# Attention-and-DHT kernel: small parameters in one packed transfer issued behind the last head, 48 instead of 64 head-dimension rows of q and k, and the low parts of the second half's relative terms subtracted on GpSimd

## The reference, cut to what matters

```python
B, H, W, C = 4, 16, 16, 192; NH = 12; HD = 16; WS = 14; MLP = 768
h = layernorm(x, ln1_g, ln1_b)                       # padded to 28 x 28, cut into 14 x 14 windows
q, k, v = split(h @ qkv_w + qkv_b)                   # 12 heads of 16 dims
rel_h = einsum('bhwc,hkc->bhwk', q, Rh)              # Rh, Rw: rel_pos_h, rel_pos_w by offset
rel_w = einsum('bhwc,wkc->bhwk', q, Rw)
scores = einsum('bqd,bkd->bqk', q, k) * HD**-0.5 + rel_h[..., :, None] + rel_w[..., None, :]
o = softmax(scores) @ v
x1 = x + (o @ proj_w + proj_b)
out = x1 + gelu(layernorm(x1, ln2_g, ln2_b) @ fc1_w + fc1_b) @ fc2_w + fc2_b
# layer 1: Hartley transform, two block-diagonal complex layers (w1, b1, w2, b2), soft threshold,
# transform back, plus the input
```

## Time and profile before

| | us |
|---|---|
| median of 3 runs | 191.21 |
| the profiled execution, its own time | 190.22 |
| its span, first to last instruction | 188.4 |
| PE busy | 175.3 |
| DVE busy | 112.9 |
| ACT busy | 87.5 |
| POOL busy | 65.7 |

### The profile page before, as it was taken

How to read it: one execution, slowest core, us unless ns; L and a number is a source line. 1 busy time by engine, 2 the same in 40 slices (tenths; PEclk the granted TensorE clock), 3 DMA queues, 4 the chain that set the end, 5 groups by cost and what they waited for, 6 DMA issues and landing times.

```text
span 188.4 us, 4169 instructions
## 1 busy us (share of the span) xinstructions
PE 175.3 (93%) x1502; PEld 153.3 (81%) x1502; DVE 112.9 (60%) x303; ACT 87.5 (46%) x230; POOL 65.7 (35%) x120
## 2 busy tenths in 40 slices
PE   7999999997998797899999999999999999999892
PEld 7766996696786675788877996878999999789892
DVE  6729675598888677587755776520111466779532
ACT  3496554934387666587785204554100223071300
POOL 1633439936055456431999521900000000000000
PEclk9999999999699999999999999999999999999999
DMA  5791227976939999957051300000012170000015
GB/s 161 210 221 25 89 79 205 225 204 180 185 105 187 218 213 205 209 115 239 12 155 41 129 0 0 0 3 0 3 43 83 42 171 0 2 0 3 0 31 138
DMA packets 12958, 19.45 MB, mean 103 GB/s; under 512 B 5197, under 2 KB 9695, under 8 KB 12938
## 3 DMA queue, kind: packets, MB, share of 16 engines
q0 software_dynamic: 3392, 10.98, 24.4%
q1 hardware_dynamic: 8810, 7.75, 17.5%
q10 hardware_dynamic: 736, 0.46, 0.9%
HBM read 6.79 MB, written 1.57 MB: 44 GB/s over the span
## 4 chain that ended last, share of the span: by engine, by line
PE 70%; DMA 9%; DVE 7%; SPq 5%; ACT 3%; issue 2%; POOL 0%; ACTq 0%; DVEq 0%; POOLq 0%
PE bank L1632 9%; PE bank L1649 8%; PE bank L1406 6%; PE bank L1474 5%; PE bank L1667 4%; DMA qop<-arena 4%; PE bank L1392 3%; SPq L607 3%; PE bank L1381 3%; PE bank L1488 3%; PE bank L1600 3%; DMA q_last<-maxt 3%; PE bank L1659 3%; PE bank L1446 3%; DMA xt<-in_x_tok 2%
## 5 line engine op out<-in xcount | busy, mean ns | idle before, releaser
L1190 DVE TENSOR_REDUCE negmax<-bank 98x2 f32<-98x392 f32 (+1 forms) x72 | 34.7, 525 | 8.8 <-PE bank L1446 8.7
L1474 PE MATMUL bank<-qop,kop 128*98 128x196 f32 (+4 forms) x140 | 22.6, 262 | 0.1
L951 ACT ACTIVATE arena<-bank 98x392 f32<-98x392 f32 x48 | 21.2, 489 | 2.5 <-PE bank L1474 2.2
L1446 PE MATMUL bank<-kop,qop 126*98 126x196 f32 x80 | 16.4, 294 | 5.3 <-DMA qop<-arena 3.8
L1474 PEld LDWEIGHTS bank<-qop,kop 128*98 128x98 f32 (+4 forms) x140 | 18.8, 176 | 0.9 <-issue 0.9
L1632 PE MATMUL bank<-h2t,wf 96*128 96x512 f32 x72 | 17.4, 398 | 0.4 <-ACT h2t L978 0.4
L1446 PEld LDWEIGHTS bank<-kop,qop 126*98 126x98 f32 x80 | 11.1, 175 | 7.3 <-issue 5.7
L1632 PEld LDWEIGHTS bank<-h2t,wf 96*128 96x128 f32 x72 | 13.3, 188 | 3.9 <-issue 0.6
L1649 PE MATMUL bank<-wf,arena 128*128 128x192 f32 x96 | 15.8, 326 | 0.0
L1649 PEld LDWEIGHTS bank<-wf,arena 128*128 128x128 f32 x96 | 15.7, 190 | 0.1
L1269 DVE TENSOR_TENSOR arena<-bank,arena 128x384 f32<-128x384 f32 x4 | 2.2, 556 | 22.1 <-PE bank L1649 22.1
(11 more groups left out here) (172 smaller groups left out, 379.5 us busy)
## 6 DMA issues: line engine op xcount, KB each, us to landing
kop<-arena POOLq DMA_DIRECT2D x20, 173.0 KB, 5.5
qop<-arena POOLq DMA_DIRECT2D x10, 227.5 KB, 6.7
qop<-arena SPq DMA_DIRECT2D x10, 130.0 KB, 2.5
qop<-arena POOLq DMA_DIRECT2D x10, 130.0 KB, 6.0
arena<-in_relw SPq DMA_DIRECT2D x2, 441.0 KB, 5.1
xt<-in_x_tok SPq DMA_DIRECT2D x4, 192.0 KB, 3.5
scratch<-arena SPq DMA_DIRECT2D x4, 192.0 KB, 2.0
k_last<-arena POOLq DMA_DIRECT2D x4, 173.0 KB, 4.8
```

Of the source, the lines that this page charges most:

```text
L951: nc.scalar.activation(pg[:, e], src[0:HWIN, 0:2 * WIN], ACT.Exp, scale=HD ** -0.5).then_inc(emptied(key), 1)
L1190: nc.vector.tensor_reduce(negmax[0:rows, n % 2, at:at + cols], ps(key)[0:rows, 0:cols * width].rearrange("p (t k) -> p t k", t=cols), AX.X ...
L1446: ins = mm(ps(key)[0:HWIN, WIN * t:WIN * t + WIN], qo(h)[0:126, c0:c0 + HWIN], ko(h)[0:126, WIN * u:WIN * u + WIN], start=True, stop=True)
L1474: ins = mm(ps(key)[0:rows, at:at + n], ko(h)[:, c0:c0 + rows], rhs, start=True, stop=True)
```

## The change

1. The 17 parameter DMAs of SP are gone. The host packs ln2, fc1_b, half4, b1, b2, w1, w2 and w2 turned into one array `params` [128, 20 + 12*24]; POOL loads it by one DMA right behind the last head's r, then `wf1_raw` and `pb`, without waiting for the last head's loads; behind that wait come `wf1_f32`, `f2b` and both rows of b2 in one DMA. Waits on `late_in` become waits on `params_in`, `pb_in` or `late_in`, each for what is used.
2. q and k have 48 rows instead of 64: the high part of q twice and the low part once, k's high and low parts and the high part again. Rows 48 to 63 are zeros: POOL sets `blank` (16 rows), and SP copies it into those rows of all five buffers of `kop` and `qop` by two DMAs before the constant rows of q, and behind a wait for `bv_in`; rows 48 to 63 of `k_last` and `q_last` are copied from there by two more DMAs between those of L611 and L612. Low times low is no longer part of the scores.
3. The relative terms of the second half: ACT writes, besides the high part, an exact copy from the bank to where the low part belongs; POOL subtracts the high part in place, one instruction over 84x1040 for each axis, the first behind `q_low_by_pool`, the second behind head 5's r. DVE's `rel_low` for f = 1 is gone.
4. `kept_busy(3)` instead of `kept_busy(6)` before `max_rows(1)`.

```diff
         def q_rows(h, part):
             f, j = h // HH, h % HH
-            src = q2[j:j + HH * (HD - 1) + 1:HH, f, part, None, :].to_broadcast([HD, 2, QN])
-            return raw(qo(h)[32 * part:32 * part + 32]), raw(src)
+            if part == 0:
+                src = q2[j:j + HH * (HD - 1) + 1:HH, f, 0, None, :].to_broadcast([HD, 2, QN])
+                return raw(qo(h)[0:32]), raw(src)
+            return raw(qo(h)[32:48]), raw(q2[j:j + HH * (HD - 1) + 1:HH, f, 1, :])
...
             sp.dma_start(relw[:, 1], a["relw"][:, 1]).then_inc(relw_in[1], 16)
+            sp.wait_ge(blank_set, 1)
+            sp.wait_ge(bv_in, 16)
+            sp.dma_start(raw(kop[48:64]), raw(blank[:, None, :].to_broadcast([16, OWN, KN]))).then_inc(blank_in, 16)
+            sp.dma_start(raw(qop[48:64]), raw(blank[:, None, 0:QN].to_broadcast([16, OWN, QN]))).then_inc(blank_in, 16)
             sp.wait_ge(qrows_set, 1)
...
-                if 2 <= h < 8:
-                    for dst, src in later_inputs[3 * (h - 2):3 * (h - 2) + 3]:
-                        sp.dma_start(dst, src, allow_slow_non_contiguous=True).then_inc(late_in, 16)
                 if h == 1:
                     sp.wait_ge(*is_full(("rel", 1, 1, 1)))
                     sp.wait_ge(q_lowered, 4)
                     sp.dma_start(raw(k_last[64:128, :]), raw(kop[64:128, 0])).then_inc(krows_set[OWN], 16)
+                    sp.dma_start(raw(k_last[48:64, :]), raw(kop[48:64, 0])).then_inc(krows_set[OWN], 16)
+                    sp.dma_start(raw(q_last[48:64, :]), raw(qop[48:64, 0])).then_inc(qrows_copied, 16)
                     sp.dma_start(raw(q_last[120:126, :]), raw(qop[120:126, 0])).then_inc(qrows_copied, 16)
...
+            nc.gpsimd.memset(raw(blank), 0.0).then_inc(blank_set, 1)
             pool.wait_ge(set_up, 6)
...
+            def r_low_by_pool(axis):
+                for p in range(2):
+                    pool.wait_ge(*is_read(("rel", 1, axis, p)))
+                nc.gpsimd.tensor_tensor(relc[:, 1, axis, 1], raw(relc[:, 1, axis, 1]), raw(relc[:, 1, axis, 0]),
+                                        ALU.subtract).then_inc(r_lowered, 1)
...
-                for copy in range(2):
-                    pool.dma_start(raw(ko(h)[32 * copy:32 * copy + 32]),
-                                   raw(k2[j:j + HH * (HD - 1) + 1:HH, f])).then_inc(k_loaded[h % NOK], 16)
+                pool.dma_start(raw(ko(h)[0:32]),
+                               raw(k2[j:j + HH * (HD - 1) + 1:HH, f])).then_inc(k_loaded[h % NOK], 16)
+                pool.dma_start(raw(ko(h)[32:48]),
+                               raw(k2[j:j + HH * (HD - 1) + 1:HH, f, 0])).then_inc(k_loaded[h % NOK], 16)
...
                         for g in range(3):
                             q_low_by_pool(g)
+                        r_low_by_pool(0)
+                    if h == OWN:
+                        r_low_by_pool(1)
                     if OWN <= h + 1 < NH:
                         load_k(h + 1)
...
+            pool.dma_start(params[:], a["params"]).then_inc(params_in, 16)
+            for c in range(2):
+                pool.dma_start(wf1_raw[:, c], a["fc1_w"][CF * c:CF * c + CF, :]).then_inc(wf1_in, 16)
+            pool.dma_start(pb[:], a["proj_b"].partition_broadcast(128)).then_inc(pb_in, 16)
             for i in range(NOP):
                 pool.wait_ge(r_loaded[i], 16 * len(range(i, HH, NOP)))
             for h in range(NH - NOK, NH):
                 pool.wait_ge(k_loaded[h % NOK], 32 * (h // NOK + 1))
-            pool.wait_ge(late_in, 17 * 16)
-            for c in range(2):
-                pool.dma_start(wf1_raw[:, c], a["fc1_w"][CF * c:CF * c + CF, :]).then_inc(wf1_in, 16)
             for c in range(2):
                 pool.dma_start(wf1_f32[:, c], a["fc1_w"][CF * c:CF * c + CF, :]).then_inc(wf1_again, 16)
+            pool.dma_start(f2b[:], a["fc2_b"].partition_broadcast(128)).then_inc(late_in, 16)
+            pool.dma_start(b2r.rearrange("p x c -> p (x c)"),
+                           a["b2"].rearrange("x n o -> (x n o)").partition_broadcast(128)).then_inc(late_in, 16)
...
                 for src, dst in rel_pieces(axis, ps(key)[0:84, :], p, relc[:, f, axis, 0]):
                     ins = nc.scalar.copy(dst, src)
-                ins.then_inc(r_high, 1)
+                if f == 0:
+                    ins.then_inc(r_high, 1)
+                else:
+                    for src, dst in rel_pieces(axis, ps(key)[0:84, :], p, relc[:, f, axis, 1]):
+                        ins = nc.scalar.copy(raw(dst), src)
+                    ins.then_inc(emptied(key), 1)
...
                 if (n, u) in K_STEPS:
                     k_low(1, K_STEPS.index((n, u)))
-                if (n, u) in R_STEPS:
-                    rel_low(1, *divmod(R_STEPS.index((n, u)), 2))
...
                         if h == OWN:
-                            pe.wait_ge(qrows_copied, 32)
+                            pe.wait_ge(qrows_copied, 48)
...
-                        pe.wait_ge(krows_set[h % NOK], 16 if h % NOK == OWN else 1)
+                        pe.wait_ge(krows_set[h % NOK], 32 if h % NOK == OWN else 1)
...
                 if h == 1:
-                    kept_busy(6, ps(key))
+                    kept_busy(3, ps(key))
...
             pe.wait_ge(qrows_copied, 16)
+            pe.wait_ge(blank_in, 32)
             for n in range(NH + 3):
```

More of the change, by code:

```diff
@@ L362, in build @@
         assert QF_AT == relw_at + 2 * WS * 84 and QF_AT + QN + KN <= vaug_at - 4 * 3 * 128
+        blank = k2[0:16, 1, 1]
         def edges(h):
@@ L709, in _ @@
                             pool.dma_start(dst, src).then_inc(q_loaded[o], 16)
-                    for axis in range(2):
-                        for p in range(2):
-                            pool.wait_ge(*is_read(("rel", f, axis, p)))
+                    if f == 0:
+                        for axis in range(2):
+                            for p in range(2):
+                                pool.wait_ge(*is_read(("rel", 0, axis, p)))
+                    else:
+                        pool.wait_ge(r_lowered, 2)
                     pool.dma_start(raw(qo(h)[64:120]),
@@ L971, in _ @@
                 outputs_read(act, nc.scalar.copy, 0, bp)
-            act.wait_ge(late_in, 17 * 16)
+            act.wait_ge(params_in, 16)
             def h2_high_part(bp):
@@ L1782, in spread, with blocks, halves @@
         return out.reshape(CF, WS, WS * HH)
[L1784 removed]
+    def blocks(w):
+        return w.reshape(2, NB // 2, BS, BS).transpose(1, 2, 0, 3).reshape(CF, 2 * BS)
+    def halves(v):
+        return v.reshape(2, CF).T
+    params = np.zeros((128, PN), np.float32)
+    params[:, 0:6] = given.pop("fc1_b").reshape(6, 128).T
+    params[0:CF, 6:10:2] = halves(given.pop("ln2_g"))
+    params[0:CF, 7:10:2] = halves(given.pop("ln2_b"))
+    params[0:CF, 10:14] = fixed.pop("half4")
+    b1, w1, w2 = given.pop("b1"), given.pop("w1"), given.pop("w2")
+    params[0:CF, 14:18] = np.concatenate([halves(b1[0]), halves(b1[1])], 1)
+    params[0:CF, 18:20] = halves(given["b2"][0])
+    turned = w2.swapaxes(2, 3)
+    params[0:CF, 20:] = np.concatenate([blocks(w) for w in (w1[0], w1[1], w2[0], w2[1], turned[0], turned[1])], 1)
+    given["params"] = params
     given["relw"] = np.stack([spread(given.pop(n)) for n in ("rel_pos_h", "rel_pos_w")], 1)
@@ L1793 @@
     given["first"][0:CF, 132:138] = given.pop("qkv_b_dj")
-    for name, v in {**given, **tables()}.items():
+    for name, v in {**given, **fixed}.items():
         arrays[f"in_{name}"] = v
```

60 lines of the change are left out of this document (26 added, 34 removed).

## The result

Median 189.14 us (18 runs, 187.71 to 190.71); the kernel before, beside it, 191.46 us (188.48 to 196.04). The ratio is 0.9919, 95% interval 0.9895 to 0.9943: 0.8% faster, where the forecast was 185.8 us, 2.8% under 191.2, with a range from 183.6 to 189.0. The profiled execution took 189.33 us with a span of 187.5, against 190.22 and 188.4 before: 0.9 us of span where the sum had 5.4. The median lies 0.14 us beyond the slow end of the range. (Each ratio leaves out executions that ran over 1.5% longer than the fastest of their kernel; medians are over all executions.)

The account below looks back on a forecast made before the run. Bounds: full DMA engines delaying q, k, r in slots 5 to 11, and DVE in slots 1 to 3. Terms -3.5 and -1.9 gave -5.4 us on a 188.4 us span, 183.0, so median 185.8 us, range 183.6 to 189.0.

Parts of the forecast that it names:

- Slots 5 to 11: Heads 5 to 11: PE's 3.8 us of waits for q, k, r loads nearly vanish; -3.5 us, ends -3.8 and -1.8.
- can't delay a head's operands: End of the heads: packed parameters and weights follow the last r on POOL's queue, so no head's operands come later.
- I cost the end of the kernel at nothing: Behind the last head: no wait of PE, DVE or ACT on the moved data becomes the later one; 0 us.
- Neither delays a load: Slots 1 to 5: POOL's two subtractions, 1.96 us each, fit its idle time; slot 5 starts 1.9 us earlier.
- the stretched split: Sign of a wrong forecast: DVE's split of the maxima stretched behind POOL's 2 us subtractions; no term in the sum.
- Head 5's constant rows: Start of slot 5: next bound, landing at 54.3 us (53.2 to 55.5), so slot 5 starts there instead of 56.16.
- Blank's copies: Start of the kernel: zeroing copies end between 18 and 24 us, before head 0's q is needed; cost nothing, 5 us cover.
- The rate of 310 GB/s: Head 0's k load into 32 rows, engines to itself; the upper rate for a 16-row copy, k then taking 0.29 us.
- rival B: Heads' loads: a 16-row copy costs as much as a 32-row one, 1.8 of 3.8 us return; 188.7 us, chance 0.11.
- C: Slot 5: PE falls to 1.2 GHz waiting for head 5, slot about 1.5 us longer; 187.3 us, chance 0.12.
- E: Heads' loads: r's landing stays at 7 us, set by issue chain and shared rings; about 189.5 us, chance 0.07.
- D: Start: zeroing copies run at 37 GB/s, the first S is 7.8 us late; 193.6 us, slower, chance 0.06.

Follow-up runs that it names:

- f_64: Changed kernel with POOL's subtractions in pieces, ScalarE copying head 5's k rows, end loads held, POOL's end work ordered, k in 64 rows: 185.57 us, ratio 0.9728.
- a_pieces: Changed kernel with each of POOL's two subtractions cut into four instructions of 260 columns: 192.87 us, ratio 1.006 to the kernel before.
- a_pc: Changed kernel with POOL's subtractions in four pieces and head 5's constant rows 64 to 127 of k copied by ScalarE: 187.68 us, ratio 0.9823.
- f_48: Changed kernel with POOL's subtractions in pieces, ScalarE copying head 5's k rows, end loads held, POOL's end work ordered, k in 48 rows: 186.96 us, ratio 0.9789.

## Why the prediction was wrong, step by step

- **Slots 5 to 11: right in the cause, and a little under.** Forecast -3.5 us, measured -4.3, beyond its end of -3.8. It named the full DMA engines, r's landing (forecast under 5, measured 4.6) and the waits. What it had not: that part 1 alone brings 0.5 us. The size is in part luck: the term rests on 682 KB for a head, and with 768.5 KB `f_64` needs 23.4 us as well.
- **Part 1, "can't delay a head's operands", "I cost the end of the kernel at nothing": failed, 1.8 us.** The step looked at q, k and r, which POOL issues ahead of the loads, and at who waits for the loaded data. It left out the last operand of a head, the maxima, 8 KB that SP issues while the loads are under way. PE goes on 4.6 and 6.1 us after their issue. The cover that I named was of POOL's wait, not of PE's.
- **Part 3, "Neither delays a load": true, and beside the point; -1.9 us forecast, about 0 measured (slots 0 to 5: -0.05).** I priced POOL's subtraction on POOL alone (1.96 us, measured 2.40) and asked whom it delays in POOL's queue. It delays DVE, through what the two engines share. I had written the stretched split among the signs that would prove me wrong, and given it no term in the sum. The Trainium skill, page "SBUF — State Buffer", section "Who interferes with whom", has the rule that I should have priced: VectorE and GpSimd share one port pair under an exclusive lock, a copy can take it in its two-port mode, and whichever engine comes second is fully blocked for the whole instruction, while a reduction never contends. The rows agree in this: 0.17 us becomes 2.80 and ends with POOL's instruction; beside pieces no instruction of the split takes over 0.64 us; six reductions beside the four pieces keep their 2.7 us. That POOL came first in slot 3 they don't show, since the copy's row begins 0.36 us before the subtraction's.
- **Head 5's constant rows: right as the next bound, wrong in its time.** Taken at 54.3 us (53.2 to 55.5), measured 57.1 in `a_pieces` and 54.9 in `a_pc`, where one of its four transfers was gone. In the changed kernel the split hid it: slot 5 at 57.76 waits for nothing.
- **Blank's copies: the rate was right (105 GB/s against 99), "nothing, with 5 us of cover" was wrong.** The cover was counted for q alone, from one landing of 2.5 us. Behind the copies q takes 8.1 us and is still in time; the operand without cover is r, on POOL's queue, at 32.4 us instead of 29.7. The price, with k's 16-row copies beside the zeroing, is 1.0 us in the changed kernel's trace and 0.6 us on average over ten kernels.
- **The rate of 310 GB/s** was read from the best half microsecond of two copies. Both together, 346 KB, are under way from 23.0 to 25.0 us, some 180 GB/s. As a whole this load runs under the ceiling that the prediction set it against, so the row speaks less against rival B than the prediction has it.
- **The rivals.** C happened in `a_pieces`. In the changed kernel the clock fell in slot 3, as before the change, behind another wait. (C's argument has a misreading: from 46.0 to 48.7 us PE was busy 1.44 of 2.70 us, about half and not a third.) E and D didn't happen (r at 4.6 us, 105 GB/s). B's price for 16 rows, equal time for half the bytes, fits `f_48` against `f_64`, but its sum has another cause. None of the five held the cause of the miss. The range left it out too: each rival moved one term, and what came was +1.65 us at the start (0.64 of them not the change's), no gain of 1.9 us in slots 0 to 5, and +1.8 us at the end, in places where the sum had zeros or a gain.

**What stays open.** How the first loss divides between the zeroing of `kop` and k's 16-row copies, and how much of the gain in slots 5 to 11 is q's rows and how much the parameters. What makes the hold of `fc1_low` differ between executions. `f_64` still has 1.4 us of waits for DVE behind `fc1_low`; another place for this instruction wasn't tried.

## What to carry to other kernels

Cost an operation moved to GpSimd against VectorE's next short instruction too: it can be held until GpSimd's instruction ends, here even through two in a row, so cut the operation into pieces, or place it where VectorE has nothing urgent. When a load is moved into a quiet stretch, look for the smallest transfer that will be issued while it is in the rings, not for the largest. And where several stalls sit in a row, follow the next bound after each removal on a trace: here one fix alone (the pieces) gave a kernel 0.6% slower than the one before the change, and together with the other edits one 2.7% faster.

## What the runs showed of the hardware that I had not expected

- A VectorE copy of 16 columns, 0.17 us alone, took 2.80 and 3.25 us beside single GpSimd instructions of 2.40 and 1.45 us (two of them in a row in the second case), and a VectorE operation of 1.0 us took 5.51 beside a chain of ten GpSimd instructions. VectorE's reductions out of PSUM kept their time: six of them took 2.73 us in `a_pieces` beside the four pieces, against 2.72 in slot 2 of the kernel before.
- SP's issue of a DMA took 3.53 us instead of 0.98 when 757 KB stood in front of it (0.87 and 0.90 behind 325 KB), and transfers of 2 and 6 KB held PE until 4.6 and 6.1 us after their issue, beside 1.7 MB of another queue.
- After a wait of 3.6 us in slot 5 the granted clock was 0.50 (1.2 GHz) for some 6 us, though PE had work all the time; behind the two waits of 1.0 us at the end of the heads the page of the changed kernel has no slice under 9 tenths.
